# Attention scores, shift and feed-forward share of a two-batch transformer layer, regrouped into two 64-row tiles of TensorE

## The reference

```
qkv = xn @ w_qkv; q, k, v split into 16 heads of 16
q, k = irfft(rfft(.) * sigmoid(mask_logits))        # a 16x16 matrix per head
attn = softmax(q k^T / 4);  attention = (attn v) @ w_out + b_out
y = square(relu(xn @ W_fc^T)) @ W_proj^T            # 256 -> 1024 -> 256
mem = 0; five times: mem = 0.9 mem + y - [mem > 1]; count [mem > 1]
feed-forward = count / 5
```

## Time and profile before

| what | value |
|---|---|
| median of three runs | 1826.79 us |
| the profiled execution | 1828.13 us |
| its span, first to last instruction | 1826.3 us |
| TensorE busy | 1811.4 us, 99% |
| VectorE busy | 1422.0 us, 78% |
| ScalarE busy | 1075.4 us, 59% |
| GpSimd busy | 710.2 us, 39% |
| mean granted clock of TensorE | 0.998 |

### The profile page before, as it was taken

How to read it: one execution, slowest core, us unless ns; L and a number is a source line. 1 busy time by engine, 2 the same in 40 slices (tenths; PEclk the granted TensorE clock), 3 DMA queues, 4 the chain that set the end, 5 groups by cost and what they waited for, 6 DMA issues and landing times.

```text
span 1826.3 us, 35321 instructions
## 1 busy us (share of the span) xinstructions
PE 1811.4 (99%) x14308; PEld 1090.5 (60%) x14308; DVE 1422.0 (78%) x1782; ACT 1075.4 (59%) x1182; POOL 710.2 (39%) x948
## 2 busy tenths in 40 slices
PE   8999999999999999999999999999999999999999
PEld 5655556666555565655555666555556665555666
DVE  6786887788778777877787778778877887788766
ACT  3435666666666666666666666666666666666662
POOL 1002334444333344443334444433344444333445
PEclk9999999999999999999999999999999999999999
DMA  5661122222202222221122222211222222112223
GB/s 178 226 205 29 34 44 43 45 45 39 41 19 39 44 43 45 43 40 33 21 45 44 43 45 39 43 28 27 45 44 44 45 39 44 24 31 44 43 79 113
DMA packets 86240, 98.82 MB, mean 54 GB/s; under 512 B 50935, under 2 KB 65015, under 8 KB 82107
## 3 DMA queue, kind: packets, MB, share of 16 engines
q1 hardware_dynamic: 82908, 93.42, 23.4%
q10 hardware_dynamic: 3168, 3.15, 0.6%
HBM read 70.80 MB, written 20.99 MB: 50 GB/s over the span
## 4 chain that ended last, share of the span: by engine, by line
PE 96%; DMA 1%; DVE 1%; SPq 0%; issue 0%; ACT 0%; ACTq 0%
PE ring L654 31%; PE banks L664 28%; PE ring L644 18%; PE banks L722 6%; PE banks L727 6%; PE banks L599 2%; PE ring L806 2%; PE ring L646 1%; PE ring L611 1%; PE ring L590 1%; DMA qk_scratch<-attnT 0%; DMA attnT<-x 0%; DMA qup<-qk_scratch 0%; DVE attnT L854 0%; PE ring L567 0%
## 5 line engine op out<-in xcount | busy, mean ns | idle before, releaser
L889 DVE TENSOR_REDUCE pmax<-ring 128x2 f32<-128x1024 f32 x1000 | 1176.9, 1218 | 332.0 <-PE ring L646 329.2
L523 ACT ACTIVATE probs<-ring 128x1024 f32<-128x1024 f32 x1024 | 993.3, 1022 | 640.0 <-PE ring L654 638.7
L654 PE MATMUL ring<-qst,kst 66*128 66x512 f32 x2048 | 614.9, 421 | 3.3 <-DMA qup<-qk_scratch 2.6
L664 PE MATMUL banks<-probs,vst 128*32 128x256 f32 x8192 | 549.0, 385 | 0.1
L654 PEld LDWEIGHTS ring<-qst,kst 66*128 66x128 f32 x2048 | 345.2, 188 | 261.2 <-issue 212.1
L644 PE MATMUL ring<-kst,qst 64*128 64x512 f32 x1000 | 387.2, 467 | 0.0
L646 PE MATMUL ring<-kup,qup 64*128 64x512 f32 x1000 | 386.7, 466 | 0.0
L664 PEld LDWEIGHTS banks<-probs,vst 128*32 128x32 f32 x8192 | 213.8, 109 | 213.7 <-issue 125.2
L435 POOL TENSOR_TENSOR lif<-lif 128x256 f32<-128x256 f32 x32 | 21.6, 676 | 795.8 <-ACT y_sb L539 795.8
L644 PEld LDWEIGHTS ring<-kst,qst 64*128 64x128 f32 x1000 | 182.9, 183 | 158.9 <-DVE pmax L889 81.9
L646 PEld LDWEIGHTS ring<-kup,qup 64*128 64x128 f32 x1000 | 182.8, 183 | 0.0
(11 more groups left out here) (76 smaller groups left out, 685.7 us busy)
## 6 DMA issues: line engine op xcount, KB each, us to landing
qup<-qk_scratch SPq DMA_DIRECT2D x252, 64.0 KB, 4.2
qst<-qk_scratch SPq DMA_DIRECT2D x124, 128.0 KB, 4.1
kst<-qk_scratch SPq DMA_DIRECT2D x62, 256.0 KB, 6.0
qk_scratch<-attnT SPq DMA_DIRECT2D x32, 256.0 KB
kup<-qk_scratch SPq DMA_DIRECT2D x64, 128.0 KB, 6.5
qk_scratch<-probs SPq DMA_DIRECT2D x16, 256.0 KB
qst<-shiftT SPq DMA_DIRECT2D x256, 2.0 KB
attnT<-o_turned SPq DMA_DIRECT2D x256, 16.0 KB, 1.9
```

Of the source, the lines that this page charges most:

```text
L523: act.activation(probs[:, s % PS, :], score_slot(g), ACT.Exp, scale=SCALE).then_inc(exp_done, 1)
L654: mm = pe.matmul(score_slot(g)[:, c * BLK:(c + 1) * BLK], kst[b][:, kt * P:(kt + 1) * P], qst[b][:, q:q + BLK], start=True, stop=True)
L664: mm = pe.matmul(po[32 * j:32 * (j + 1), half * D:(half + 1) * D], vst[b][:, kt, :], quarters[:, j], start=(kt == 0), stop=(kt == TB - 1))
L889: dve.tensor_reduce(pmax[:, tile, first:first + 2], unit_slot(g).rearrange("p (c e) -> p c e", c=2), AX, ALU.max).then_inc(mx_taken, 1)
```

## The change

The scores keep only 64 rows. The stacks `qst` and `kst` get 128 partitions: rows 64 to 127 are a full copy of rows 0 to 63, and `qup` and `kup` go. The step with the even number uses rows 0 to 63, the odd one rows 64 to 127. The shift is added by matmuls of its own: `ones` against `shift_rows`, whose rows 0, 1 and 64, 65 hold the shift and whose others are zero, 64 rows again. The feed-forward calls are halved along their contraction: one call on rows 64 to 127 and one on rows 0 to 63, added up in PSUM, the upper one first (`upper_share`). `pair` has a new order, the slots are given out anew, the units of maxima come in another order, and the stack of a unit is loaded by 12 larger DMAs. The first unit's stack goes to its own buffers, the stack of unit 1 in two pieces, since `qst[1]` and `kst[1]` serve the first maxima.

```
+STACK = 12 * 16
+SHIFT = 8 * 16
 ...
         def score_slot(g):
-            return ring[:, (4 * (g // 2) + g % 2) % 3, :]
+            return ring[:, (4 * (g // 2) + 1 + g % 2) % 3, :]
         def unit_slot(g):
-            return ring[:, (4 * (g // 2) + 2 + g % 2) % 3, :]
+            return ring[:, (4 * (g // 2) + 3 * (g % 2)) % 3, :]
 ...
+            def load_stack(h, b, cols, landed):
+                tok = slice(b * S + cols.start, b * S + cols.stop)
+                for side in range(2):
+                    for part in range(2):
+                        for dup in range(2):
+                            r = side * SIDE + (2 * part + dup) * DH
+                            sp.dma_start(qst[b][r:r + DH, cols].bitcast(F32), qk_dram[0, h, part, :, tok]).then_inc(landed, 16)
                     for dup in range(2):
+                        r = side * SIDE + dup * 2 * DH
+                        sp.dma_start(kst[b][r:r + 2 * DH, cols].bitcast(F32),
+                                     qk_dram[1, h, :, :, tok].rearrange("r d t -> (r d) t")).then_inc(landed, 16)
 ...
+            def store_shift(n, half):
                 sp.wait_ge(shift_turned, n + 1)
+                for side in range(2):
+                    dst = shift_rows[side * SIDE:side * SIDE + 2, cols].rearrange("r (t j q) -> r t j q", j=4, q=32)
 ...
                 if t == 5:
+                    load_stack(0, 0, slice(0, S), stack_in[0])
 ...
+            sp.wait_ge(mx_ready, FIRST_MAX)
+            load_stack(0, 1, slice(0, HALF), second_in[0])
+            load_stack(0, 1, slice(HALF, S), second_in[1])
 ...
+                if i and not last:
+                    sp.wait_ge(exp_done, STEPS * i + 2)
+                    load_stack(h + b, 1 - b, slice(0, S), stack_in[1 - b])
 ...
+            def scores(g, s, b, side, c):
+                pe.matmul(score_slot(g)[:, c * BLK:(c + 1) * BLK], kst[b][rows_of(side), kt * P:(kt + 1) * P],
+                          qst[b][rows_of(side), q:q + BLK], start=True, stop=False)
+            def shifted(g, s, side, c):
+                mm = pe.matmul(score_slot(g)[:, c * BLK:(c + 1) * BLK], ones[rows_of(side), :],
+                               shift_rows[rows_of(side), q:q + BLK], start=False, stop=True)
+                if c == 1:
+                    mm.then_inc(score_ready, 1)
 ...
+            def score_free(x):
 ...
+                elif x % 2:
+                    pe.wait_ge(mx_taken, taken(x - 2))
+                else:
+                    pe.wait_ge(exp_done, x + 2)
 ...
+            def pair(h, b, s, last=False, share=None, between=None):
+                if ahead:
+                        pe.wait_ge(exp_done, g + 1)
+                    if s == LEAD and i:
+                        pe.wait_ge(stack_in[mb], STACK * (h + 2 * b))
+                    maxima(g, s, mb)
+                if scored:
+                    score_free(g)
+                    if share:
+                        scores(g, even, sb_, 0, 0)
+                        share(1, 0)
+                        scores(g, even, sb_, 0, 1)
+                        share(1, 1)
+                        shifted(g, even, 0, 0)
+                        score_free(g + 1)
+                        scores(g + 1, odd, sb_, 1, 0)
+                        shifted(g, even, 0, 1)
+                        scores(g + 1, odd, sb_, 1, 1)
+                        share(0, 0)
+                        shifted(g + 1, odd, 1, 0)
+                        share(0, 1)
+                        shifted(g + 1, odd, 1, 1)
 ...
                 if ahead:
+                    pe.wait_ge(mx_taken, taken(g))
+                    maxima(g + 1, s + 1, mb)
                 for v in (s - LAG, s - LAG + 1):
```

More of the change, by code:

```diff
@@ L718, in pair, with up, down @@
                         times_v(STEPS * i + v, v % STEPS, b if v < STEPS else 1 - b)
-            def up(tile, f):
+            def up(tile, f, side, c):
+                return pe.matmul(misc[:, (f % 4) * P:(f % 4 + 1) * P], wfc_sb[rows_of(side), c, f * P:(f + 1) * P],
+                                 xnT[rows_of(side), c, tile * P:(tile + 1) * P],
+                                 start=(side == 1 and c == 0), stop=(side == 0 and c == KC - 1))
+            def down(f, side):
+                return pe.matmul(misc[:, 0:D], hid_sb[rows_of(side), f, :], wproj_sb[rows_of(side), f, :],
+                                 start=(f == 0 and side == 1), stop=(f == FC - 1 and side == 0))
@@ new lines, in head, with share @@
+            def head(h, b, last=False):
+                i = 2 * h + b
+                def share(s, side, c):
+                    opens, ends = (side, c) == (1, 0), (side, c) == (0, 1)
+                    if opens:
+                        pe.wait_ge(score_ready, STEPS * i + s)
+                    if (side, c) == (0, 0):
+                        pe.wait_ge(upper_share, TB * i + (s - FIRST) // 2 + 1)
+                    if s in (6, 8):
+                        mm = up(i, 6 + (s - 6) // 2, side, c)
+                        if ends and s == 8:
+                            mm.then_inc(misc_full, 1)
+                    if s == 10 and opens:
+                        pe.wait_ge(misc_taken, use(i, DOWN))
+                        pe.wait_ge(squared, 2 * i + 3)
+                        if i == 0:
+                            pe.wait_ge(wproj_in, 16)
+                    if s == 18 and opens:
+                        pe.wait_ge(squared, 2 * i + 4)
+                    if 10 <= s <= 24 and c == 0:
+                        mm = down((s - 10) // 2, side)
+                        if side == 0 and s == 24:
+                            mm.then_inc(misc_full, 1)
+                    if s == 26 and opens:
+                        pe.wait_ge(misc_taken, use(i, UP_A))
+                    if s == 34 and opens:
+                        pe.wait_ge(misc_taken, use(i, UP_B))
+                    if s >= 26:
+                        mm = up(i + 1, (s - 26) // 2, side, c)
+                        if ends and s == 32:
+                            mm.then_inc(misc_full, 1)
+                    if side == 1 and c == (0 if 10 <= s <= 24 else 1):
+                        mm.then_inc(upper_share, 1)
+                for s in range(FIRST, STEPS + FIRST, 2):
+                    pair(h, b, s, last, (lambda side, c: share(s, side, c)) if s <= 24 or not last else None)
@@ L885, in unit_max @@
             def unit_max(g, s):
[L886 to L887 removed]
+                tile, part = unit_of(s)
                 dve.wait_ge(mx_ready, FIRST_MAX + g + 1)
[L889 removed]
+                dve.tensor_reduce(pmax[:, tile, 2 * part:2 * part + 2],
                                   unit_slot(g).rearrange("p (c e) -> p c e", c=2), AX, ALU.max).then_inc(mx_taken, 1)
```

239 lines of the change are left out of this document (87 added, 152 removed).

## The result

| | us |
|---|---|
| before, median of 4 runs | 1827.02 (1826.24 to 1829.41) |
| after, median of 4 runs | 1952.00 (1948.24 to 1953.04) |
| ratio, 95% interval | 1.0676 (1.0663 to 1.0688) |
| after, the profiled execution and its span | 1950.97, 1949.1 |

The change costs 125 us; 86 were forecast. From the page of the kernel after: its busy times, then its chain by engine and by line.

A forecast was written before the change was run, and what follows sets the result against it. ScalarE's and VectorE's loops bound it: ten pairs at 3.24 and six stalled ones, plus 0.3 for loads, 55.3 us a unit against 52.40. Sum 87 + 0.8 - 4 + 2 = +86: 1913 us, own range 1870 to 1958.

The forecast's parts named there:

- TensorE's path of 3.03: TensorE's own work in a pair, the two row tiles fully overlapping: 3.03 us, against 3.275 a pair before.
- in order: Rival: both row tiles keep program order on TensorE, a pair takes 3.59 us, kernel about 2020; chance 0.10.
- no overlap: Rival: matmuls of different types do not overlap on TensorE, 3.90 us a pair, kernel 2135; chance 0.06.
- ScalarE's loop of 3.24: Scores wait for the exponential whose slot they take; this loop sets an ordinary pair at 3.24 us.
- VectorE's loop: Second maxima wait for the first's reduction through the shared slot: 2.95 us a pair plus VectorE's other work.
- X of the VectorE stalls: VectorE's work between second reduction and next pair's first: shift 0.98 us, normalisation 1.04, output 0.44.
- The loads: A unit's stack takes 14.5 us to load; TensorE waits 1.0 us at step 8, net 0.3 a unit.
- ScalarE's copies "cost nothing": ScalarE's relu and y copies fall in its 1.3 us of idle time a pair, at no cost.
- Clock: Rival: the 1.0 us wait at each step 8 lowers TensorE's clock, +78 us, kernel 1990; chance 0.10.
- Faster: Rival: neither loop closes and TensorE's 3.03 decides, -122 us, kernel 1705; chance 0.09 with what lies between.
- First unit: Step 8's DMA wait and half clock go (-5.2), VectorE stalls add 1.6; stack in full queue +2 (0 to +8).
- Last unit: After the maxima end, TensorE's pair stays 2.56 us as before; just +0.8 us from steps 34 to 36.

The follow-up runs named there:

- gp_halfboth: gp with half of each exponential on ScalarE and half of each maxima reduction on VectorE left out: 1708.6 us, ratio 0.9346.
- oneside: gp_halfboth with the odd step's scores and shift on rows 0 to 63 as well: 2183.8 us, ratio 1.1946.
- gp_halfmax: gp with each maximum taken over half of the keys, so VectorE's reductions are shorter: 1835.8 us, ratio 1.0044.
- gp_halfexp: gp with the exponential taken of the first 512 columns of each slot only: 1822.1 us, ratio 0.9971.
- gaps: The changed kernel with VectorE's extra work cut into parts and moved behind the even step's reduction: 1924.3 us, ratio 1.0537.
- pieces_lif: pieces with GpSimd's last `acc` addition held until VectorE's normalisation multiplication is done: 1906.4 us, ratio 1.0431.
- pieces: The changed kernel with every unit's stack loaded in two pieces with their own semaphores: 1921.2 us, ratio 1.0511.
- relu: gps with ScalarE's two feed-forward copies given to VectorE and the first shift links moved to step 11: 1823.0 us, ratio 0.9972.
- gp: The changed kernel with the edits of gaps and pieces together: 1845.6 us, ratio 1.0102.
- gps: gp with the load of `wproj` issued behind the first piece of unit 1's stack: 1841.7 us, ratio 1.0080.

## Why the prediction was right, and where its sizes were off

The direction held, the two mechanisms that were forecast are in the trace, and 1952 lies in the forecast's own range, 6 us under its upper end. The time came out 39 us over the forecast, and a second loop and ScalarE's copies were missing from it. By its own steps:

- **TensorE's path of 3.03: right.** gp_halfboth runs at 3.03, oneside at 0.92 more. The rivals "in order" (3.59) and "no overlap" (3.90) fall, and the calls on the two sides do run side by side. The pair shown above has a shift matmul start ahead of one that stands before it in the program. The Trainium skill, "TensorE: Matmul & The Clock Gate", section "Part 3: Packing small matmuls", has matmuls start and end strictly in program order; by it the pair would not have been below 3.59, and the runs disagree: each row tile went through its own list.
- **ScalarE's loop of 3.24: right in size, but not the only one.** It measures 3.22 alone (gp_halfmax). The loop from the first maxima over their reduction to the second maxima and the values is 3.25. The prediction closed VectorE's loop from reduction to reduction (2.95) and had 0.54, 1.22 and 0.05 at hand, but did not set the sum, 1.82, against TensorE's 1.71 between the two maxima. That the time is hardly other for it (3.25 for 3.24) is luck: the two loops happen to be equally long. A remedy for ScalarE alone would have bought little, as gp_halfexp shows.
- **X of the VectorE stalls: right, a little too large.** 3.29, 3.85 and 3.80 for 3.39, 3.99 and 3.93: -0.37 a unit. The run gaps takes these three away. The exception is step 4, with 4.36 for 3.99, because of GpSimd's addition, as pieces_lif shows. The Trainium skill, "SBUF — State Buffer", section "SBUF: two separate sides", tells of a port pair that VectorE and GpSimd share, taken by one for a whole instruction while the other is blocked; the 0.82 beside 0.29 agrees. In the changed kernel the 0.5 should cost nothing of its own, since the loads end the same stretch; this is argued, not run.
- **The loads: the mis-sized term.** The last lands 15.3 us after the first issue (median of the 30 units, 14.8 to 16.2), not 14.5. The pairs of steps 0 to 6, which these loads end, take 15.6 together, not 14.9: +0.7 a unit, some 22 us of the 39. The load also covers the stalls in that stretch, which is why gaps and pieces gave so little alone. The rate in the full stretch is 169 to 180 GB/s; the prediction had taken 206 for the second half.
- **ScalarE's copies "cost nothing": wrong.** The pair of step 10 has 0.2 more, and that of step 2 takes 3.58, of which VectorE explains only 3.29, the value of its twin at step 18; in gaps it stays at 3.57. TensorE needs the feed-forward's bank in the middle of the scores, before the exponentials of that pair can start, and the copy stands behind those of the pair before. The run relu takes both stalls away. Where a VectorE stall has just stretched a pair, the copy has time: in pieces step 10 takes 3.26, behind a step 8 of 3.81.
- **Clock: as forecast for 29 of the 30 waits** (1.00). Behind the one of 1.95 us it fell to 0.50, and in gaps it did so at 11 of 30. The rival's mechanism is real: it cost about 1.2 us here, and 14 us one edit away.
- **"Faster": fell,** for the reason given (X above 0.08), and because even without stalls the pair stands at 3.25. The run gp, with nearly all stalls gone, is still 1% slower than the kernel before.
- **First unit: wrong.** -2 was forecast for start and first unit together, +6.1 was measured. The step at 8 lost its 2.6 us wait, but the first scores come 7.3 us later. "+2 (0 to +8)" for the stack in a full queue had the place right and the size wrong: 5.95 us of idle time, then half clock with pairs of 5.03 and 5.08. The shift is ready at 108.07 and stands in SyncE's queue until 116.67; its eight issues take 6.0 us and the scores start 4.7 later. In gps the issues ended 4.7 earlier than in gp, and so did the scores start. That the queue stands because the DMA engines are full is argued from their share of 1.03 over the four issues ahead.
- **Last unit: +2.4 for +0.8.** One pair, that of step 10, takes 3.72 for 2.56, without any maxima. Timeline of the kernel after:

```profile
1888.55 0.60 ACT L526 ACTIVATE relu_sb<-banks 128x512 f32<-128x512 f32 x1
...
1889.25 0.45 PE L767 MATMUL banks<-wproj_sb,hid_sb 64*128 64x256 f32 x1 [0.69 <-issue]
```

  The feed-forward's upper half (L767) waits until the copy has ended, and the scores behind it wait too. It is ScalarE's copy again, +1.2; in relu the same pair takes 2.56. The stalls at steps 2 and 4 (3.58 and 4.36) make +1.4, where +0.8 was forecast; step 6 gives back 0.4 and step 28 adds 0.2.

Summed for a unit against 55.3: loads +0.7, step 10 +0.2, ordinary pairs +0.1, the three stalls -0.4, and 0.1 at the pair of step 8 and in rounding: 56.1 by medians, 56.19 by the mean. What stays open is the stretch of 4.7 to 5.2 us between the last issue of the first shift and the first scores.

## What to carry to other kernels

When two steps begin to share a buffer, write down every loop through it, also the one that goes through another engine and back inside the same step, and compare each with the engine's own path between the same two points; equal loops mean that no single remedy pays. Stalls that lie under one wait are not additive: take the wait away first, or expect each remedy alone to give a fraction. Work that must go somewhere belongs behind the instruction after which its engine waits anyway, and a copy that frees a bank belongs on the engine that isn't queued behind the work which the bank's next writer feeds.

## What the runs showed of the hardware

- A VectorE multiplication with two SBUF inputs that started 0.06 us after the start of a GpSimd addition took 0.82 us in place of 0.29, and ended 0.15 after the addition's end. Its recorded length contains the wait.
- Matmuls on rows 0 to 63 and on rows 64 to 127 overlap wholly, float32 beside float32r too, and each side keeps its own order only: 3.03 a pair with both sides (gp_halfboth), 3.95 with four matmuls moved to one (oneside).
- TensorE's granted clock stood at 1.00 behind 29 waits of 0.54 to 1.88 us and was 0.50 for 3.4 us behind one of 1.95. In gaps it was 0.50 at 11 waits of 1.96 to 2.99 and 1.00 at 19 of 1.49 to 2.69, so the length of the wait alone does not decide it. Behind one of 5.95 it was 0.50 over 5.1 us.
- With the DMA engines full (1.03), four DMA issues of one queue took 16.45 us, one of them 11.67, against 0.46 for the one before them. What waited for eight transfers of 2 KB started 4.7 to 5.2 us after their last issue, from SyncE's queue and from ScalarE's alike.
